# Six of 24 row tiles of a mixture of experts added to a table of token sums in DRAM

## What is computed

```
buf = zeros((E, CAP + 1, H)).at[se, slot].set(x[tok])[:, :CAP]
h = silu(einsum('ech,ehf->ecf', buf, w_gate)) * einsum('ech,ehf->ecf', buf, w_up)
out = einsum('ecf,efh->ech', h, w_down)
gathered = out[se, minimum(pos, CAP - 1)] * valid[:, None]
return segment_sum(gathered * w, tok, num_segments=Tn)
```

## Time and profile before

| | |
|---|---|
| median of 3 runs | 431.84 us (431.19 to 432.56) |
| the profiled execution | 430.28 us, span 428.3 us |
| PE | 399.0 us busy, 93% of the span |
| DVE | 352.2 us, 82% |
| ACT | 220.5 us, 51% |
| POOL | 118.8 us, 28% |
| scatter matmuls L1668 | 192, 52.0 us busy |
| indirect gathers L420 | 24, 26.3 us busy |
| chain that ended last | PE 49%, DVE 40%, ACT 3% |
| granted PE clock | 0.995 of full over the span |

### The profile page before, as it was taken

The page is one execution under the profiler, slowest core; times in us unless marked ns, Lnnn a source line. Parts: engine busy times, 40 slices in busy tenths (PEclk is TensorE's granted clock), DMA queues, the critical chain, the costliest instruction groups (busy, mean ns, idle before and its releaser), DMA issues.

```text
span 428.3 us, 5191 instructions
## 1 busy us (share of the span) xinstructions
PE 399.0 (93%) x1711; PEld 216.3 (50%) x1715; DVE 352.2 (82%) x655; ACT 220.5 (51%) x410; POOL 118.8 (28%) x85
## 2 busy tenths in 40 slices
PE   5899999899998789989999999999999999998795
PEld 2244545687655557767777754344444344333241
DVE  4999999898699889999979799437977977638996
ACT  3976838742484468646668564511111141146892
POOL 2722007000000563321200000337684845540000
PEclk9999999999999999999999999999999999999899
DMA  7950001900096459767764510720000000000002
GB/s 262 399 219 2 2 0 35 390 5 2 9 346 189 98 140 314 214 213 253 233 215 142 201 51 1 300 93 2 0 0 1 0 2 0 0 0 0 1 2 98
DMA packets 12251, 47.45 MB, mean 111 GB/s; under 512 B 2897, under 2 KB 5434, under 8 KB 9794
## 3 DMA queue, kind: packets, MB, share of 16 engines
q1 hardware_dynamic: 11074, 43.20, 28.7%
q0 software_dynamic: 1152, 3.93, 3.8%
HBM read 44.76 MB, written 2.37 MB: 110 GB/s over the span
## 4 chain that ended last, share of the span: by engine, by line
PE 49%; DVE 40%; issue 4%; ACT 3%; DMA 1%; another core or an unknown queue 1%; POOL 1%; POOLq 0%; SPq 0%; DVEq 0%; ACTq 0%
PE bank L1668 8%; PE bank L1804 8%; PE bank L1791 6%; PE bank L1724 4%; PE bank L1836 4%; PE bank L1833 4%; PE bank L1697 3%; PE bank L1635 2%; DVE wkv_b L806 2%; DVE wkv_b L795 2%; DVE wkv_a L795 2%; PE bank L1759 2%; PE bank L1566 2%; DVE wkv_c L773 1%; DVE wkv_a L806 1%
## 5 line engine op out<-in xcount | busy, mean ns | idle before, releaser
L730 ACT ACTIVATE early<-bank 128x512 f32<-128x512 f32 (+1 forms) x24 | 14.3, 597 | 86.0 <-PE bank L1804 76.6
L1668 PE MATMUL bank<-onehot,rows 128*128 128x512 f32 x192 | 52.0, 410 | 0.0
L1307 DVE TENSOR_TENSOR early<-early,bank 128x512 f32<-128x512 f32 (+1 forms) x24 | 16.4, 684 | 36.2 <-ACT early L730 32.8
L420 POOL DMA_INDIRECT arena<-token_rows,arena x24 | 26.3, 1098 | 62.8 <-PE bank L1706 32.7
L1804 PE MATMUL bank<-arena 128*128 128x512 f32 (+1 forms) x96 | 42.2, 600 | 0.1
L431 POOL TENSOR_TENSOR early<-early,arena 128x512 f32<-128x512 f32 (+1 forms) x12 | 20.1, 1672 | 76.0 <-DMA arena<-pair_weights 67.8
L1668 PEld LDWEIGHTS bank<-onehot,rows 128*128 128x128 f32 x192 | 34.0, 188 | 11.0 <-issue 4.1
L1791 PE MATMUL bank<-cT,arena 128*128 128x512 f32 x80 | 37.9, 596 | 0.0
L437 POOL TENSOR_TENSOR early<-early,arena 128x512 f32<-128x512 f32 x10 | 22.3, 2231 | 28.2 <-DVE early L1307 28.2
L1804 PEld LDWEIGHTS bank<-arena 128*128 128x128 f32 (+1 forms) x96 | 15.7, 181 | 22.6 <-issue 20.7
L1697 PE MATMUL bank<-arena 128*64 128x192 f32 x256 | 22.5, 329 | 2.3 <-issue 2.3
(11 more groups left out here) (399 smaller groups left out, 893.6 us busy)
## 6 DMA issues: line engine op xcount, KB each, us to landing
arena<-in_w_gateup SPq DMA_DIRECT2D x16, 768.0 KB, 7.7
arena<-in_w_down SPq DMA_DIRECT2D x8, 768.0 KB, 10.5
arena<-in_wq SPq DMA_DIRECT2D x1, 2048.0 KB
arena<-in_wo SPq DMA_DIRECT2D x1, 2048.0 KB, 8.0
const<-in_const SPq DMA_DIRECT2D x1, 1688.0 KB, 10.5
arena<-in_w_upgate SPq DMA_DIRECT2D x1, 1408.0 KB, 5.8
kT<-in_kT SPq DMA_DIRECT2D x2, 512.0 KB, 5.6
xT<-in_xT SPq DMA_DIRECT2D x1, 1024.0 KB, 8.8
```

The lines of the kernel that those rows point to most:

```text
L420: g.indirect_dma_start(xg[:, t % XRING, :], None, scratch[:, :], bass.IndirectOffsetOnAxis(ap=toki[:, t:t + 1].bitcast(U32), axis=0)).then ...
L1668: return mm(bank[2 * ct + ch][:], rows1[:, i % RRING, part, ct * P:(ct + 1) * P], onehot1[:, t, ch * CHUNK:(ch + 1) * CHUNK], start=False, ...
```

## The change

Tile 0 of groups 0 to 5 (`ADDED`) no longer goes through `rows1`, one-hot and scatter matmuls. The other 18 tiles (`PLACED`) do as before, with ring positions counted over them alone.

A table `expert_sums` lies in DRAM, 128 x 16 rows of 256 floats: token t has row (t mod 128) * 16 + t div 128. POOL clears it early, in the attention of layer 0, by a memset of 2304 columns and a DMA, and waits for that. DVE computes the row numbers of the slots of tile 0 (`sumrow`), slots without a token get a spare row of their own in each partition; for that PE makes three more products, and DVE five small operations. When the outputs of tile 0 are in `outw`, POOL issues three indirect DMAs that add them to the table, one for each expert's part of the tile (48, 48 and 32 rows; within one expert no token stands twice), and waits before each until the one before has landed. `add_rows(g)` comes after the gathers of group g + 4. ACT takes the tiles of groups 0 to 5 in the order 1, 2, 0, writes tile 0 only to `outw`, and waits in groups 1 to 6 before tile 0 until the adds of the group before have landed. When all are in, SP reads the first 8 rows of each partition back (1 MB, `sums1`), and PE adds them into banks 0 to 3 by 16 float32 products with the identity before the last group's scatter.

The diff, without the moves of buffers, one more column of constants (`spare`, 16 p), the new last count of the semaphore that releases the adds to `x`, and one semaphore of layer 2 that takes the place of another:

```diff
@@ -56,6 +56,10 @@
 RRING = 4
+ADDED = tuple((g, 0) for g in range(6))
+PLACED = [(g, t) for g in range(NG) for t in range(GT) if (g, t) not in ADDED]
+PIECES = tuple((lo, min(lo + CAP, P)) for lo in range(0, P, CAP))
+SUMROWS = 16
 LOW = -1e30
...
@@ -136,6 +141,8 @@
         scratch = nc.dram_tensor("token_rows", [N + 1, ROW], F32, kind="Internal").ap()
+        sums = nc.dram_tensor("expert_sums", [P * SUMROWS, C], F32, kind="Internal").ap()
+        sum_rows = sums.rearrange("(p r) c -> p (r c)", r=SUMROWS)
         pair_weights = nc.dram_tensor("pair_weights", [2, N], F32, kind="Internal").ap()
...
@@ -270,6 +279,14 @@
+        def out_order(g):
+
+            return (1, 2, 0) if (g, 0) in ADDED else (0, 1, 2)
+
+        def out_count(g, t):
+
+            return GT * g + out_order(g).index(t) + 1
+
         def tail2(it):
...
@@ -330,6 +347,8 @@
+            sp.wait_ge(S("sums_added"), 16 * (1 + len(PIECES) * len(ADDED)))
+            sp.dma_start(sums1.rearrange("p t c -> p (t c)"), sum_rows[:, 0:NT * C]).then_inc(S("rows_out"), 16)
             sp.wait_ge(S("ffn1_done"), NG - 1)
...
@@ -395,6 +414,9 @@
+            step(g.memset(zeros, 0.0))
+            g.dma_start(sum_rows[:, 0:(NT + 1) * C], zeros).then_inc(S("sums_added"), 16)
+            pool.wait_ge(S("sums_added"), 16)
             for j in range(6):
...
@@ -406,20 +428,39 @@
             pool.wait_ge(S("rows_out"), 48)
-            for t in (*range(GT, 2 * GT), *range(GT), *range(2 * GT, ST)):
-                if t == 0:
-                    pool.wait_ge(S("xgT_done"), 1)
-                    for i in range(2):
-                        last = g.memset(xgT[i][:, :, GS:XW], 0.0)
-                    last.then_inc(S("pads_ready"), 1)
-                if t % GT == 0 and t >= 2 * GT:
-                    pool.wait_ge(S("h1_turned"), 2 * max(t // GT - 2, 1))
-                if t >= XRING:
-                    pool.wait_ge(S("xgT_done"), (t - XRING) // GT + 1)
-                    pool.wait_ge(S("wslot_ready"), (t - XRING) // GT + 1)
-                g.indirect_dma_start(xg[:, t % XRING, :], None, scratch[:, :],
-                                     bass.IndirectOffsetOnAxis(ap=toki[:, t:t + 1].bitcast(U32), axis=0)
-                                     ).then_inc(S(f"gather{t // GT % 4}"), 16)
+
+            def gathers(g1):
+                for t in range(g1 * GT, (g1 + 1) * GT):
+                    if t >= XRING:
+                        pool.wait_ge(S("xgT_done"), (t - XRING) // GT + 1)
+                        pool.wait_ge(S("wslot_ready"), (t - XRING) // GT + 1)
+                    g.indirect_dma_start(xg[:, t % XRING, :], None, scratch[:, :],
+                                         bass.IndirectOffsetOnAxis(ap=toki[:, t:t + 1].bitcast(U32), axis=0)
+                                         ).then_inc(S(f"gather{g1 % 4}"), 16)
+
+            def add_rows(g1):
+
+                pool.wait_ge(S("toki_ready"), 3)
+                pool.wait_ge(S("outw_ready"), out_count(g1, 0))
+                for k, (lo, hi) in enumerate(PIECES):
+                    pool.wait_ge(S("sums_added"), 16 * (1 + len(PIECES) * g1 + k))
+                    g.indirect_dma_start(sums[:, :], bass.IndirectOffsetOnAxis(ap=sumrow[0:hi - lo, k * NG + g1:k * NG + g1 + 1], axis=0),
+                                         outw[lo:hi, 0, :], None, compute_op=ALU.add).then_inc(S("sums_added"), 16)
+
+            gathers(1)
+            pool.wait_ge(S("xgT_done"), 1)
+            for i in range(2):
+                last = g.memset(xgT[i][:, :, GS:XW], 0.0)
+            last.then_inc(S("pads_ready"), 1)
+            gathers(0)
+            pool.wait_ge(S("h1_turned"), 2)
+            gathers(2)
+            gathers(3)
+            for g1 in range(len(ADDED)):
+                if g1 + 4 < NG:
+                    pool.wait_ge(S("h1_turned"), 2 * (g1 + 2))
+                    gathers(g1 + 4)
+                add_rows(g1)
...
@@ -680,16 +721,20 @@
-                for t in range(GT):
+                for t in out_order(g):
                     i = g * GT + t
                     act.wait_ge(S("ffn1_done"), g + 1)
                     act.wait_ge(S("wslot_ready"), g + 1)
-                    if g >= 1:
-                        act.wait_ge(S("rows1_ready"), i - GT + 1)
-                    if i >= RRING:
-                        act.wait_ge(S("scat1_done"), i - RRING + 1)
+                    if (g - 1, t) in ADDED:
+                        act.wait_ge(S("sums_added"), 16 * (1 + len(PIECES) * g))
+                    elif g >= 1:
+                        act.wait_ge(S("rows1_ready"), PLACED.index((g - 1, t)) + 1)
                     row = bank[6 + t // 2][:, (t % 2) * C:(t % 2 + 1) * C]
-                    s.activation(rows1[:, i % RRING, 0, :], row, ACT.Copy, scale=wslot[:, i:i + 1])
+                    if (g, t) in PLACED:
+                        n = PLACED.index((g, t))
+                        if n >= RRING:
+                            act.wait_ge(S("scat1_done"), n - RRING + 1)
+                        s.activation(rows1[:, n % RRING, 0, :], row, ACT.Copy, scale=wslot[:, i:i + 1])
...
@@ -1094,6 +1139,8 @@
                             float(N), float(N), ALU.add, ALU.min).then_inc(S("toki_ready"), 1)
+            v.tensor_scalar(sumtok, bank[4][0:CAP, ST:2 * ST], float(N), float(N), ALU.add, ALU.min)
+            step(v.tensor_scalar(sumrow, bank[4][0:CAP, ST:2 * ST], 0.0, spare[0:CAP], ALU.is_ge, ALU.mult))
             v.tensor_scalar(tokf.rearrange("p (g t) -> p t g", t=GT), slots, float(N), float(N), ALU.add, ALU.min).then_inc(S("toki_ready"), 1)
...
@@ -1104,6 +1151,9 @@
             shared_product(1)
+            step(v.tensor_scalar(sumbits, sumtok, P - 1, 4, ALU.bitwise_and, ALU.logical_shift_left))
+            step(v.scalar_tensor_tensor(sumrow, sumtok, 7, sumrow, ALU.logical_shift_right, ALU.bitwise_or))
+            v.tensor_tensor(sumrow, sumrow, sumbits, ALU.bitwise_or).then_inc(S("toki_ready"), 1)
             back_again(2, 0, 0, near=1)
...
@@ -1116,18 +1166,18 @@
-                i = g * GT + t
-                if g >= 1:
-                    dve.wait_ge(S("scat1_done"), i - GT + 1)
+                i, n = g * GT + t, PLACED.index((g, t))
+                if n >= GT:
+                    dve.wait_ge(S("scat1_done"), n - GT + 1)
                 else:
                     dve.wait_ge(S("xgT_done"), 1)
-                v.tensor_scalar(onehot1[:, t, :], iota, tokf[:, i:i + 1], None, ALU.is_equal).then_inc(S("onehot1_ready"), 1)
+                v.tensor_scalar(onehot1[:, n % GT, :], iota, tokf[:, i:i + 1], None, ALU.is_equal).then_inc(S("onehot1_ready"), 1)
 
             def slot_rest(g, t):
 
-                i = g * GT + t
-                dve.wait_ge(S("outw_ready"), i + 1)
-                v.tensor_tensor(rows1[:, i % RRING, 1, :], outw[:, t, :], rows1[:, i % RRING, 0, :].bitcast(F32),
+                n = PLACED.index((g, t))
+                dve.wait_ge(S("outw_ready"), out_count(g, t))
+                v.tensor_tensor(rows1[:, n % RRING, 1, :], outw[:, t, :], rows1[:, n % RRING, 0, :].bitcast(F32),
                                 ALU.subtract).then_inc(S("rows1_ready"), 1)
...
@@ -1180,9 +1230,11 @@
                 for t in range(GT - 1):
-                    slot_onehot(g, t)
+                    if (g, t) in PLACED:
+                        slot_onehot(g, t)
                 for t in range(GT):
-                    slot_rest(g, t)
+                    if (g, t) in PLACED:
+                        slot_rest(g, t)
...
@@ -1642,6 +1694,8 @@
                           start=True, stop=True)
+            for k in range(len(PIECES)):
+                last = mm(bank[4][0:CAP, ST + k * NG:ST + (k + 1) * NG], spreadv[:, k, :], groups1[:], start=True, stop=True)
             last.then_inc(S("counts1_done"), 1)
...
@@ -1662,16 +1716,24 @@
-                i = g * GT + t
-                pe.wait_ge(S("onehot1_ready"), i + 1)
-                pe.wait_ge(S("rows1_ready"), i + 1)
-                return mm(bank[2 * ct + ch][:], rows1[:, i % RRING, part, ct * P:(ct + 1) * P],
-                          onehot1[:, t, ch * CHUNK:(ch + 1) * CHUNK], start=False, stop=(i == ST - 1 and part == 1))
+                n = PLACED.index((g, t))
+                pe.wait_ge(S("onehot1_ready"), n + 1)
+                pe.wait_ge(S("rows1_ready"), n + 1)
+                return mm(bank[2 * ct + ch][:], rows1[:, n % RRING, part, ct * P:(ct + 1) * P],
+                          onehot1[:, n % GT, ch * CHUNK:(ch + 1) * CHUNK], start=False, stop=((g, t) == PLACED[-1] and part == 1))
+
+            def sums_to_banks(ct):
+
+                pe.wait_ge(S("rows_out"), 64)
+                for t in range(NT):
+                    mm(bank[2 * ct + t // 4][:, t % 4 * P:(t % 4 + 1) * P], sums1[:, t, ct * P:(ct + 1) * P], ident,
+                       start=False, stop=False, skip_group_check=True)
 
             def scatter_run(g, first, n):
 
-                for k in range(first, first + n):
```

(26 more changed lines are left out.)

## The result

The changed kernel takes 492.3 us (488.2 to 495.5, 4 runs) against 432.2: ratio 1.140, interval 1.134 to 1.146. Slower, as forecast, but by 60 us and not by 30; the range of 440 to 482 missed it. The two profiled executions lie 64.8 us apart (495.04 and 430.28), the medians 60.1; the traces can split only the former.

A forecast was written before the change was run, and what follows sets the result against it. PE, busy 93%, bounded the kernel; the change adds a loop of waits. Four loops +28.2, ahead +0.7, tail +1.4: +30.3 on 430.28 gives 460.6, or 462.1 from the median; forecast 461 us, own range 451 to 471, wide range 440 to 482.

The forecast's parts named there:

- The closed loop: Groups 0 to 3, through POOL, DMA, ACT, DVE and PE: 20.05 us each, four taking 80.2 against 52.0 before.
- The gathers: Loop step on POOL: from U to the end of three gathers, after which the adds begin; 4.2 us.
- U: Moment when both halves of a group's hidden rows are turned, read as the start of ACT's second copy of that group.
- S: Loop step of three indirect adds, each issued after the one before has landed: 11 us, own range 9 to 13.
- beside a ring load: Add rounds during SP's load of expert weights: two of three, 4.0 us each with the gap; the third 3.0.
- The isolated price: Software DMA meeting no load: a gather of 128 rows in an empty queue landed 2.8 us after issue.
- rival 1: Short add rounds, lengthened by neither load nor DRAM: 2.5 us each, S = 7.5, loop 16.05, total 442 us; 26%.
- From eviction to the next U: Loop steps on ACT: tile 0 eviction with wake 0.6, then 3.75 to the next U, 0.5 for PE's clock.
- The tail: From U(5) to the end of the scatter and new products: 39.0 us against 37.6 before, +1.4.
- Ahead of the stage: Preparation before layer 1's routed experts, three products and small DVE operations: +0.7 us, from 0.3 to 1.5.
- The upper rival: Second rival: add rounds of 5.3 us each behind ring packets and two DRAM trips, PE's clock falling; S = 16, 486 us; 15%.
- rival 3: Faster: an add lands within 1.25 us, S = 3.75; 428 us, at best 423 were the adds free; 6%.

The follow-up runs named there:

- the run with 13: Changed kernel with 13 extra f32 matmuls of 512 columns (zero weights) on PE before the first turn of hidden rows in groups 2 to 5: 485.8 us (1.127).

## Why the prediction was right in kind and wrong in size

- *The closed loop* was right: waits of ACT before tile 0 in groups 1 to 4 and in no other tile, PE and DVE standing with it, 18 new issues in threes. Exchanging two steps of it took away half the loss, and opening it took away 39 us.
- *The gathers*: 4.2 us forecast from U to the first add; 168.19 - 164.04 = 4.15 measured, and 4.4 to 4.7 in the other groups. In four loops, 1 us.
- *S, the three adds, is the term that was mis-sized*: 11 forecast; 16.7, 15.7, 16.2 and 16.4 measured from the first add to ACT's eviction. Of its three rounds the one "beside a ring load" failed. The prediction had the right row, a gather of 7.0 us beside a load, and discounted it to 4.0 for the fewer rows. The round took 9.0 to 10.1, longer than the gather's 7.0 with its full 128 rows. The discount asked how much the DMA itself moves; what decides is when the load is over, for which the prediction had 8.5 us from the earlier trace rows. On the other hand mostly one round met the load, not two, because it lasted nearly as long as the load. The isolated rounds were 3.3, against 3.0. S cost 4 x 5.2 = 21 of the 34.6 us that were missed (64.9 - 30.3).
- *The isolated price* was right: the gather landed 2.8 us after its issue, the adds that met no load mostly 2.8 to 3.1, with a wake of 0.3 behind it; rival 1's 2.5 a round was too low. The Trainium skill's 2.1 us by estimate (DMA: Bandwidth & Descriptors, "Anatomy of one DMA — SWDGE (gpsimd) path") agrees with this case's copies, which landed mostly after 2.1 to 2.5 us where they met no load, and is 0.7 to 1.0 below the adds. The sum that followed from it, 439, is 53 us off; 25 of them are the load's, by the run without loads. The prediction calls short rounds "the second rival's mechanism"; it is the first rival's.
- *From eviction to the next U*: 4.75 forecast with the eviction and half a microsecond for the clock; 5.9, 4.5, 5.8, 5.8 measured. The clock's part is 1.4, nearly three times what I took. In four loops the step missed by 3 us.
- *The tail*: +1.4 forecast, +9.3 measured. The adds of group 5 hold ACT 5.8 us where 2.8 were forecast, PE stalls before U(7) and drops to 1.2 GHz again (0.50 in 294 to 300), and the products took 3.5, not 2.4: a float32 product stands in the profile as two instructions of 0.11 us, a transpose of the earlier trace rows, from which I had the price, as one.
- *Ahead of the stage*: +0.7 forecast, +1.3 measured. *After it*: 1.6 that I had at nothing. The two traces differ there in the granted clock, 0.83 against 0.91 in the stretch from 140 to 160 us behind the end of the scatter; no run tests whether that is the cause.
- *The upper rival* (S = 16, 486 us) had the sum of the three rounds and the clock's fall; it had 15%. Its mechanism was half right: it had three rounds of 5.3 us each, where one took 9.6 and two 3 to 3.5, and the addition is no second long trip. The argument against it, "the load is over before the third round", was true and beside the point.
- *The base*: rivals 1 and 2 (442, 486) are counted from the profiled execution, rival 3 (428, at best 423) from the median of the runs; from the same base it would be 427 and 422.

## What to carry to other kernels

A DMA on which a queue waits is not priced by its bytes alone: ask what transfer the same event starts elsewhere. Here an add of 48 KB that began with a load of 2.25 MB ended within 0.6 us of the load in three groups of four, so the load's full time was the price to take. Three small DMAs in turn, each waited for, cost here 10 us alone and 16 beside a load, more than the 2 us of matmuls that they replaced. Before moving work to an idle engine's queue, follow who waits behind it; the order of two steps in POOL's queue was worth 30 us, and the idea at its best 3, with two thirds of the readback left out.

## What the runs showed of the hardware

An indirect add of 48 rows of 1 KB to DRAM takes 3.3 us from issue to the next issue and lands after 3.0 to 3.1, a copy of the same rows 2.5 to 2.9, landing after 2.2 to 2.6, where no load is at its height (single ones took 0.6 more). POOL's instruction is 1.36 us of the one and 0.88 of the other. The same add issued 0.3 to 1.0 us after a load of 2.25 MB took 9 to 10 us, beside a third of that load 6.4 on average; in one group its packets began 5.6 us after its issue, against 1.9 alone. PE's granted clock, with no work on PE since 173.1, was 0.96 of full in 176 to 178 and 0.50 from there until after 190. Fillers of matmuls on zero weights kept it at 2.4 GHz through the waits before U(2) to U(5), but for one stretch of the run with 13, in which the filler ended 3 us before the wait did (0.50 in 236 to 238).
